# Fills written as 32-bit words chunk by chunk, the first keys fetched from ScalarE's queue, and the recurrence begun on half a chunk

## What is computed

```python
# layer 0
qkv = ln(x) @ w_qkv.T                      # 16 heads of 16
x += softmax(mask(q @ k.T * scale)) @ v @ w_proj.T
x += cross_attention(ln(x), ctx) @ Wo      # 77 keys
x += sum_e gate[e] * (ln(x) @ We[e] + be)  # 8 experts, top 2 by weight
# layer 1
xi = ln(x) @ Wi.T + bi
h = tanh(xt + h @ Wh.T + bh)               # lax.scan over the 1024 positions
x += hs
x += cross_attention(ln(x), ctx) @ wo + bo
x += gated experts (512 shared and 16 x 64 routed hidden units)
```

## Time and profile before

| | us |
|---|---|
| median of 3 runs | 1586.08 |
| lowest and highest of them | 1584.55, 1588.29 |
| the profiled execution's own time | 1593.49 |
| its span, from first to last instruction | 1591.9 |

### The profile page before, as it was taken

One profiled execution on the slowest core, in us unless ns is written; L12 is line 12 of the kernel. 1 busy time (PEld: TensorE's weight loads), 2 busy tenths in 40 slices (PEclk: granted clock), 3 DMA queues, 4 the chain that ended last, 5 costly groups with the idle time before them and its releaser, 6 DMA issues.

```text
span 1591.9 us, 49074 instructions
## 1 busy us (share of the span) xinstructions
PE 1529.6 (96%) x20210; PEld 1055.7 (66%) x20210; DVE 821.7 (52%) x2568; ACT 595.8 (37%) x2778; POOL 38.1 (2%) x60
## 2 busy tenths in 40 slices
PE   5498799999999999999999999999999999999998
PEld 4365267766777776767777777776766667666555
DVE  6746734387751179665212555753464433633264
ACT  1133151624237732422777555212522235322220
POOL 1100000000000000000000000000000000000000
PEclk9699789999999999999999998999989999999999
DMA  7324100110000020000001131000000010000100
GB/s 215 68 88 85 31 2 1 24 36 3 2 2 3 12 41 9 2 2 2 9 4 30 62 103 30 1 1 2 16 2 2 15 36 2 2 2 19 31 1 14
DMA packets 45472, 40.23 MB, mean 25 GB/s; under 512 B 9723, under 2 KB 44486, under 8 KB 45254
## 3 DMA queue, kind: packets, MB, share of 16 engines
q1 hardware_dynamic: 45254, 37.11, 9.9%
HBM read 25.81 MB, written 10.80 MB: 23 GB/s over the span
## 4 chain that ended last, share of the span: by engine, by line
PE 91%; DVE 6%; DMA 1%; issue 1%; ACT 0%; SPq 0%; DVEq 0%; ACTq 0%
PE b L509 20%; PE b L528 12%; PE b L1583 8%; PE b L1363 7%; PE b L1635 6%; PE b L993 5%; PE b L964 4%; PE b L734 4%; PE b L909 3%; PE b L690 3%; DVE mx L918 3%; PE b L1244 3%; PE b L1219 2%; PE b L451 2%; PE b L645 2%; PE b L493 1%
## 5 line engine op out<-in xcount | busy, mean ns | idle before, releaser
L509 PEld LDWEIGHTS b<-hp,whp 128*128 128x128 f16 x12276 | 481.0, 96 | 251.0 <-ACT hp L554 147.9
L509 PE MATMUL b<-hp,whp 128*128 128x2 f16 x12276 | 534.4, 165 | 2.0 <-DVE hp L560 0.8
L560 DVE TENSOR_TENSOR hp<-hist,hp 128x4 f16<-128x4 f32 x1023 | 165.7, 162 | 494.2 <-ACT hist L555 484.5
L554 ACT ACTIVATE hp<-b 128x4 f16<-128x4 f32 x1024 | 178.8, 175 | 536.6 <-PE b L509 525.0
L528 PE MATMUL b<-whp 128*128 128x512 f16 (+7 forms) x1038 | 256.0, 348 | 0.0
L918 DVE TENSOR_REDUCE mx<-b 128x1 f32<-128x512 f32 (+3 forms) x304 | 188.2, 657 | 5.4 <-PE b L912 4.8
L978 ACT ACTIVATE vp<-b 128x512 f32<-128x512 f32 x288 | 170.6, 603 | 25.0 <-PE b L967 13.3
L555 ACT ACTIVATE hist<-b 128x4 f32<-128x4 f32 x1024 | 178.8, 175 | 0.0
L1583 PE MATMUL b<-vp,heads 128*128 128x512 f16 x576 | 164.4, 379 | 0.0
L1363 PE MATMUL b<-we,xT 128*128 128x256 f32 x512 | 126.6, 391 | 0.0
L909 PE MATMUL b<-heads 128*128 128x512 f16 (+3 forms) x384 | 112.8, 332 | 7.1 <-DVE mx L918 3.7
(11 more groups left out here) (202 smaller groups left out, 1594.6 us busy)
## 6 DMA issues: line engine op xcount, KB each, us to landing
x_qs<-qx_scr SPq DMA_DIRECT2D x48, 128.0 KB
qx_scr<-xq_pair SPq DMA_DIRECT2D x16, 256.0 KB, 2.1
heads<-q_scr SPq DMA_DIRECT2D x24, 128.0 KB, 4.4
heads<-k_scr SPq DMA_DIRECT2D x48, 64.0 KB, 2.5
x<-in_x SPq DMA_DIRECT2D x8, 256.0 KB, 6.1
we<-in_L_ffn_We SPq DMA_DIRECT2D x2, 1024.0 KB
q_scr<-tail SPq DMA_DIRECT2D x8, 256.0 KB, 3.3
k_scr<-tail SPq DMA_DIRECT2D x8, 256.0 KB, 2.2
```

The source lines that it names most:

```text
L509: return pe.matmul(self.z(t)[:, m], self.w.whp[:, a, k, m * P:(m + 1) * P], self.g.hp16[:, (t - 1) % 2, part, k, :], start=False, stop=Tru ...
L554: act.activation(self.g.hp16[:, t % 2, 0], self.z(t), ACT.Tanh, scale=1 / LIFT).then_inc(self.s["hi_ready"], 1)
L560: v.tensor_tensor(self.g.hp16[:, t % 2, 1], self.g.hist[:, :, :, t % (4 * HALF)], self.g.hp16[:, t % 2, 0], ALU.subtract).then_inc(self.s[ ...
```

## The change

- **Fills.** Ones for the keys are written as 32-bit words (`ONES16` is the float whose bits are two 16-bit ones), in 8 memsets of 1024 words, one for each chunk and batch row, in place of 4 memsets of 4096 16-bit elements; `load_k` of chunk c waits for the fills of chunks 0 to c alone. The cross attention's key zeros and query ones are words too. The values' ones (`fill_v`) go only to the columns that need them. Small rows are filled first; the fills of later chunks and the cross attention's come after the first chunk's fourth `qk_part2`.
- **Transfers.** The 12 transfers of the first chunk's keys are issued from ScalarE's queue. Four kinds of SyncE's transfers (the weights of the recurrence and of the experts, the second layer's, and the cross attention's key rows and keys) are placed behind them in the plan.
- **Recurrence.** `start` waits for two stored tiles and does the products of half 0 alone; half 1 gets its 12 pieces inside the steps of half 0, every eighth step as the later halves do.
- **Ranks.** Norm, projections and values of layer 0 rank at 200c (AHEAD) in place of 1000c. n3 and its store rank at 45, before the experts' 50, not behind them at 60. The first pass may be at most 3 banks ahead of `self_highest` (FIRST_BANKS).
- Costs in the planner's list are adjusted to the above.

The diff, without the lines that only give names to the 32-bit views:

```diff
+FIRST_BANKS = 3
+AHEAD = 200
+
+ONES16 = (1 + 0x3C00 / 2 ** 23) / 2 ** 7
...
         self.piece_at = {HALF * (h - 1) + 16 + 8 * i + (1 - parity): (h, parity, m, k, i)
-                         for h in range(2, NH) for i, (parity, m, k) in enumerate(self.pieces)}
-        self.clear_at = {HALF * (h - 1) + 2 + parity: (h, parity) for h in range(2, NH) for parity in range(2)}
+                         for h in range(1, NH) for i, (parity, m, k) in enumerate(self.pieces)}
+        self.clear_at = {HALF * (h - 1) + 2 + parity: (h, parity) for h in range(1, NH) for parity in range(2)}
         st.ops["pe"]["idle"] = self.idle
-        st.add("pe", "start", self.start, 1, 6.0, lambda i: rank)
+        st.add("pe", "start", self.start, 1, 3.0, lambda i: rank)
...
     def start(self, pe, _):
-        pe.wait_ge(self.norm.s["stored"], 4)
+        pe.wait_ge(self.norm.s["stored"], 2)
         pe.wait_ge(self.w.s["lifted"], 1)
         pe.wait_ge(self.w.s["b_in"], 1)
         pe.wait_ge(self.w.s["row_in"], 1)
-        for h in range(2):
-            for parity, m, k in self.pieces:
-                last = self.inject(pe, h, parity, m, k, first=h == 0 and m == 0 and k == 0)
+        for parity, m, k in self.pieces:
+            last = self.inject(pe, 0, parity, m, k, first=m == 0 and k == 0)
         last.then_inc(self.s["started"], 1)
...
         if t - 2 in self.clear_at:
             h, parity = self.clear_at[t - 2]
-            pe.wait_ge(self.s["zeroed"], 2 * (h - 2) + parity + 1)
+            pe.wait_ge(self.s["zeroed"], 2 * (h - 1) + parity + 1)
...
-        if h in (3, 4):
+        if h == 3:
             act.wait_ge(self.s["started"], 1)
-        if h >= 5:
-            act.wait_ge(self.s["injected"], h - 4)
+        if h >= 4:
+            act.wait_ge(self.s["injected"], h - 3)
...
-        self.proj = Projection(st, "qk", 2 * KD, xT, [(c, w, ln) for c in range(NK)], block, rank, room.pair)
+        self.proj = Projection(st, "qk", 2 * KD, xT, [(c, w, ln) for c in range(NK)], block, lambda c: AHEAD * c + 10, room.pair)
...
-        st.add("pe", "self_v", self.make_v, 2 * NH * KD, 0.43, lambda i: chunk_of_tile(i // KD) + 0.095,
+        st.add("pe", "self_v", self.make_v, 2 * NH * KD, 0.43, lambda i: AHEAD * (i // KD // TC) + 10.095,
                opens=lambda i: ("self_v", i // KD) if i % KD == 0 else None)
-        st.add("act", "self_vkeep", self.keep_v, 2 * NH, 0.38, lambda j: chunk_of_tile(j) + 0.12,
+        st.add("act", "self_vkeep", self.keep_v, 2 * NH, 0.38, lambda j: AHEAD * (j // TC) + 10.12,
                closes=lambda j: ("self_v", j))
-        st.add("sp", "self_load_q", self.load_q, NK, 5.0, lambda c: rank(c) + 0.21, after=8.0)
-        st.add("sp", "self_load_k", self.load_k, NK, 7.5, lambda c: rank(c) + 0.21, after=8.0)
+        st.add("sp", "self_load_q", self.load_q, NK, 4.4, lambda c: rank(c) + 0.21, after=8.0)
+        st.add("act", "self_load_k0", lambda act, _: self.load_k(act, 0), 1, 7.0, lambda _: rank(0) + 0.21, after=6.0)
+        st.add("sp", "self_load_k", lambda sp, i: self.load_k(sp, i + 1), NK - 1, 7.5, lambda i: rank(i + 1) + 0.21,
+               after=8.0, behind=[("self_load_k0", lambda i: 1)])
         st.add("pe", "self_first", self.first_pass, len(self.items),
                lambda i: self.items[i][2] * (0.0535 * self.items[i][4] + 0.01) + 0.06 * self.items[i][2] * self.is_diagonal(i),
-               lambda i: chunk_of_tile(self.items[i][0]) + 0.22, opens=lambda i: ("self_first", i))
+               lambda i: chunk_of_tile(self.items[i][0]) + 0.22, opens=lambda i: ("self_first", i),
+               behind=[("self_highest", lambda i: i - FIRST_BANKS + 1)])
...
-        sp.wait_ge(self.w.s["ks_ones"], 2 * B)
+        sp.wait_ge(self.w.s["ks_ones"], B * (c + 1))
...
-        st.add("v", name + "_zero", self.zero, 2, 1.2, early, behind=first)
-        st.add("v", name + "_one", self.one, 4, lambda i: (0.4, 1.0, 1.0, 0.4)[i], lambda i: early(i // 3), behind=first)
+        st.add("v", name + "_zero", self.zero, 2, 1.4, early, behind=first)
+        st.add("v", name + "_one", self.one, 4, lambda i: (0.5, 1.2, 1.2, 0.5)[i], lambda i: early(i // 3), behind=first)
...
-        st.add("sp", name + "_rows_k", self.rows_k, 2, 5.2, early, after=4.0)
-        st.add("sp", name + "_load_k", self.load_k, 2 * B, 3.8, lambda i: early(i // B), after=5.0)
+        st.add("sp", name + "_rows_k", self.rows_k, 2, 5.2, early, after=4.0, behind=later)
+        st.add("sp", name + "_load_k", self.load_k, 2 * B, 3.8, lambda i: early(i // B), after=5.0, behind=later)
...
-        v.memset(self.layers[layer].ks.rearrange("p b h t -> p (b h t)"), 0.0).then_inc(self.s["zeroed"], 1)
+        v.memset(self.layers[layer].ks_words, 0.0).then_inc(self.s["zeroed"], 1)
...
-            v.memset(self.qs[:, half * (i - 1):half * i].rearrange("p h n -> p (h n)"), 1.0).then_inc(self.s["oned"], 1)
+            v.memset(self.qs[:, half * (i - 1):half * i].rearrange("p h n -> p (h n)").bitcast(F32), ONES16
+                     ).then_inc(self.s["oned"], 1)
...
-        ln1 = ChunkNorm(st, "n1", lambda i: (g.x_in[i // TC], 32), tile_rank(0, 0), xn1,
+        ln1 = ChunkNorm(st, "n1", lambda i: (g.x_in[i // TC], 32), lambda j: j // TC * AHEAD, xn1,
...
-                               lambda n: when(*order[n]) + 30, cross_room, [("fill", lambda i: 2)])
+                               lambda n: when(*order[n]) + 30, cross_room, [("fill", lambda i: 7), ("qk_part2", lambda i: 4)],
+                               [("self_load_k0", lambda i: 1)])
...
-        ln3 = ChunkNorm(st, "n3", lambda i: (experts.s["mixed"], (E0 + 1) * (i + 1)), tile_rank(0, 60),
+        ln3 = ChunkNorm(st, "n3", lambda i: (experts.s["mixed"], (E0 + 1) * (i + 1)), tile_rank(0, 45),
...
         def fill(v, i):
-            if i < 2:
-                v.memset(attn.qs[:, H // 2 * i:H // 2 * i + H // 2].rearrange("p h n -> p (h n)"), 0.0
-                         ).then_inc(s["qs_zeros"], 1)
-            elif i < 6:
-                b, half = (i - 2) // 2, (i - 2) % 2
-                v.memset(attn.ks[:, b, H // 4 * half:H // 4 * (half + 1)].rearrange("p h n -> p (h n)"), 1.0
-                         ).then_inc(s["ks_ones"], 1)
-            elif i == 6:
+            if i == 0:
                 v.memset(rw.lift_row[:], LIFT).then_inc(s["row_in"], 1)
-            elif i == 7:
+            elif i == 1:
                 v.memset(wx0.ones16[:], 1.0).then_inc(s["rows"], 1)
+            elif i == 2:
+                v.memset(wx1.one_row[:], 1.0).then_inc(s["row_in"], 1)
+            elif i < 5:
+                v.memset(heads[:, 8192 + 2048 * (i - 3):8192 + 2048 * (i - 2)], 0.0).then_inc(s["qs_zeros"], 1)
             else:
-                v.memset(wx1.one_row[:], 1.0).then_inc(s["row_in"], 1)
+                c, b = (i - 5) // B, (i - 5) % B
+                v.memset(heads[:, 4096 * b:4096 * (b + 1)].rearrange("p (r t) -> p r t", r=H // 2)[
+                    :, :, P * c:P * (c + 1)], ONES16).then_inc(s["ks_ones"], 1)
 
         def fill_v(v, i):
-            if i < 2:
-                v.memset(attn.va[:, NT // 2 * i:NT // 2 * (i + 1)].rearrange("p t w -> p (t w)"), 1.0
+            if i == 0:
+                v.memset(attn.va[:, :, 0:H * VW].rearrange("p t (h w) -> p t h w", w=VW)[:, :, :, DH], 1.0
                          ).then_inc(s["va_ones"], 1)
+            if i == 1:
+                v.memset(attn.va[:, :, H * VW:VP], 1.0).then_inc(s["va_ones"], 1)
...
-        st.add("sp", "load", load, 5, 2.0, lambda i: -3900 + 100 * i, after=5.0)
-        st.add("sp", "load_second", load_second, 3, 2.5, lambda i: (-3400, 190, 990)[i], after=5.0)
+        st.add("sp", "load", load, 5, 2.0, lambda i: -3900 + 100 * i, after=5.0,
+               behind=[("self_load_k0", lambda i: int(i > 2))])
+        st.add("sp", "load_second", load_second, 3, 2.5, lambda i: (-3400, 190, 990)[i], after=5.0,
+               behind=[("self_load_k0", lambda i: 1)])
         st.add("sp", "load_whole", load_whole, 2, 0.7, lambda j: 1000, after=12.0)
-        st.add("v", "fill", fill, 9, lambda i: (1.95, 1.95, 1.95, 1.95, 1.95, 1.95, 0.1, 0.1, 0.1)[i], lambda i: 10.12,
-               behind=[("fill_v", lambda i: 2)])
-        st.add("v", "fill_v", fill_v, 4, lambda i: (2.0, 2.0, 0.3, 0.3)[i], lambda i: 2)
+        st.add("v", "fill", fill, 5 + B * NK, lambda i: 0.2 if i < 3 else 2.0 if i < 5 else 1.1,
+               lambda i: 1.0 if i < 3 else 10.12 if i < 7 else 70.0,
+               behind=[("qk_part2", lambda i: 4 if i >= 7 else 0)])
+        st.add("v", "fill_v", fill_v, 4, lambda i: (0.4, 0.4, 0.3, 0.3)[i], lambda i: 2)
...
-        st.add("act", "n1_store", store1, 2 * NH, 0.35, tile_rank(0, 0.7), closes=lambda i: ("n1", i))
+        st.add("act", "n1_store", store1, 2 * NH, 0.35, lambda j: j // TC * AHEAD + 0.7, closes=lambda i: ("n1", i))
...
-        st.add("act", "n3_store", rnn.store_input, 2 * NH, 0.35, tile_rank(0, 60.7), closes=lambda i: ("n3", i))
```

(1 more changed line is left out.)

11 lines of the change are left out of this document (7 added, 4 removed).

## The result

The changed kernel takes 1571.54 us (median of 4 runs, 1566.34 to 1574.74). The kernel before took 1587.18 beside it (4 runs, 1584.55 to 1590.94). The ratio is 0.9897, with a 95% interval of 0.9862 to 0.9931: faster by 16 us, where the forecast said 42. The profiled execution took 1570.91 us, its span is 1569.2.

The account below looks back on a forecast made before the run. It took the end to be set by chunk 3 passing layer 0 (1057 us), then 367 steps and 129 us, with a 20 us hole at the head. 28 + 8 + 8 - 2 = 42 us off 1586.1 gave 1544, range 1528 to 1560.

Parts of the forecast that it names:

- The rival of the moved hole: After 82 us new lists leave new holes; only about a third of the sum arrives: 12 us, 1574 us; 13%.
- The three gains: Earlier head 28 us, half a chunk first 8 us, and the first pass's bank limit 8 us.
- the 2 that were taken off for costs: Less room ahead of VectorE in first passes and two more PSUM clears at steps 2 and 3: 2 us lost.
- Nothing in it has a date of its own: Line of chunks from 82 to 1057 us: each released by the one before, so the head's 28 us survive.
- head: Faster fills and earlier key loads bring the first maximum from 81.77 to 49 us; 28 us at the end.
- half chunk first, with n3's rank: Step 657 released 14.2 us earlier because two stored tiles suffice; bounds 0 and 14 us, 8 taken.
- banks: First pass limited to 3 of 5 banks, so experts of chunks 1 and 2 begin earlier; 8 us, at most 24.7.
- the sign given for the banks: In the profile after, fillers under 10 us in both stretches ahead of the experts of chunks 1 and 2.
- the weights in the way of the keys: Rival: 2.6 MB of weights pass before the first keys land; head gives 18 in place of 28, 1554 us; 12%.
- The start on half a chunk: First tanh 14 to 19 us earlier, worth nothing at the end because the break at step 145 absorbs it.
- The slower rival: First pass with 3 banks starves, VectorE waits at each maximum; gain gone or time up to 1623 us; 5%.
- the signs to look for: Profile after: key loads 34 to 44 us, first maximum 46 to 52, first tanh 225 to 240, step 657 1000 to 1025.

Follow-up runs that it names:

- the head alone and the guard moved: Changed kernel with ranks, bank limit, n3 and recurrence start as before, and the wait for the second layer's cross-attention values moved to step 102: 1565.64 us, ratio 0.985.
- the same head: Changed kernel keeping only the new fills and transfers; ranks, bank limit, n3 and recurrence start as before, wait still ahead of step 0: 1617.22 us, ratio 1.0179.
- 1559.73: Changed kernel with projections ranked at 1000c, no bank limit, and the wait for the second layer's values moved to step 102: 1559.73 us, ratio 0.983.
- the version at 1554.51: Changed kernel with layer 0's norm, projections and values ranked at 1000c again, all else as changed, three banks included: 1554.51 us, ratio 0.9802.
- two banks and the guard moved: Changed kernel with ranks at 1000c, two banks for the first pass, and the wait for the second layer's values moved to step 102: 1544.1 us, ratio 0.9733.
- the weights early: Changed kernel with the weights of the recurrence and experts not placed behind the first key loads: 1568.19 us, ratio 0.9869.
- the run with two banks: Changed kernel with ranks at 1000c and two banks for the first pass instead of three: 1544.61 us, ratio 0.9746.

## Why the forecast was wrong

**The failed step** is a term put at nothing without a reason: the ranks at 200c stand in the change and have no place in "28 + 8 + 8 - 2 = 42". They cost 17 us (1571.54 against 1554.51), and the intervals of the two ratios are apart. The rows that go with it are those of chunk 1: projections of later chunks stand between its first-pass products. The rival of the moved hole gave 1574 and came nearest. Its reason against itself, that projections "rank behind chunk 0's own work", looked at the wrong chunk: chunk 1's first pass ranks at 1000 and more, and projections of chunks 2 and 3 at 410 and 610 pass it.

The rest of the error is one of sizes. The three gains measure 33 us for 44 forecast, so 42 less 16 is made up of 17 for the ranks and 11 for the gains, less the 2 that were taken off for costs.

**"Nothing in it has a date of its own"** was the reason for letting the head's gain pass whole through the line of chunks. For the lists with the head alone and the guard moved it comes out: 23 us are gained at the first maximum (58.4 for 81.8), 25 and 26 at the last scores of chunks 2 and 3, and 27 at step 657. As a statement on the kernel it is false all the same. By the guard the recurrence can't begin before the projections of the last chunk are made, and with the guard in its place the same head gives 1617 us. In the kernel before, the last self values were made at 140 us and the second layer's values at 146, long ahead of the first tanh at 277.9; so the wait never showed in its trace, and could be read only in the code. That they were early because TensorE had nothing else to do in the hole that the change closes is likely by the order of the lists, but no run shows it. In the changed kernel the guard is not what costs the 17 us. The ranks at 200c do a real thing there: they keep the projections in time for the guard. But the limit of three banks does it too, and both together are one too many.

**The other terms:**

| term | forecast | measured |
|---|---|---|
| head | 28 | 22.2 (1587.86 - 1565.64), guard moved |
| half chunk first, with n3's rank | 8 | 5.9 (1565.64 - 1559.73), guard moved; not apart from 0 by the intervals |
| banks | 8 | 15.6 with two (1559.73 - 1544.1), guard moved; about 5 with three (1559.73 - 1554.51), not apart from 0 |
| ranks at 200c | none | -17.0 (1554.51 - 1571.54) |

With three banks that is 22 + 6 + 5 - 17 = 16 us. It must come out so, because each row begins where the one above it ends; the sum is a way of sharing out the 16 us and no proof. Its third step also crosses from the guard moved to the guard in its place. That should cost little, since step 657 has a break of 44 us in the version at 1554.51, and moving the guard changed nothing with two banks. A term depends on the lists that it is measured in, so the table is one order of the edits and not a law: n3's rank is worth 17.7 us in one pair of lists and -5 in another (1566.54 against 1571.54, the intervals overlap). Two of the forecast's terms were also weaker than they looked. The middle of 0 and 14 less 1 is 6, not 8. And the sign given for the banks, fillers under 10 us ahead of the experts of chunks 1 and 2, did not come: they are 14.59 us from 380 to 410 and 13.14 from 650 to 680.

No term stood for the granted clock. Its median was 0.973 in the kernel before, 0.977 to 0.978 in the changed one, 0.982 with the head alone and the guard moved, and 0.985 with two banks and the guard moved. At 1.5 us for each 0.001, an estimate, a good half of the head's 22.2 us and of the 15.6 us of two banks goes with the clock. TensorE stood idle and at 0.50 from 40 to 60 us before, so a part of that is the hole itself. How much of the rest is an effect of the order of work, no run shows.

**The head's size.** The first maximum was forecast for 49 and came at 60.1 (57.0 with the weights early), 21.7 us earlier than before and not 32.8. The keys account for 3 us of this: the last of them was issued at 39.4 and had landed by 49.7 at the latest, for 46.5 forecast. The rest is in TensorE's list. Its products for the second layer's keys (L63) stand ahead of chunk 0's first pass and wait until 57.9 for the second layer's bias, which SyncE issues only at 51.18, behind the weights of the experts (its two transfers hold the queue for 4.54 us from 40.33) and of the second layer (one of them holds it for 4.25 us). This load was placed behind the keys by the change itself, and I had given that no price. Ahead of it VectorE and ScalarE also sit 5.1 and 4.8 us on the weights of the recurrence, ahead of the norms that they have to do. With the weights early the bias is issued at 40.13 and the first maximum comes at 57.0, so the same wait is shorter and not gone.

The Trainium skill ("DMA: Bandwidth & Descriptors", Issuing engines are not separate DMA queues) says that transfers started by several engines run on the same 16 DMA engines and interleave, and that a second queue saves only the time of issuing. The rows fit that, with the engines busy 1.00 from 40 to 60 and landings of 8.3 us for 2.4, but no run shows it by itself. The rival that the forecast built on it, the weights in the way of the keys, is refuted as it stood: with the weights long landed the keys took 7.7 us at the median, and the first maximum gained 3 us, not 10.

**The half chunk.** The start on half a chunk was priced at nothing and is worth nothing (1569.93 against 1571.54). The two expert tiles that now come behind step 657 were feared to cost up to 14 us, and the 405 us after it are the same as before. The fillers did not give the room, as the forecast had it: they are 78.5 us for 79.55. In that stretch 11.6 us of expert products (36 of L1371) are new, and 24 products of layer 1's gated experts, 6.1 us, lie elsewhere; the stretch's clock was 0.98 for 0.97.

**The slower rival**, a first pass starved by three banks, is refuted by the run with two banks, the fastest but for the moved guard. A slower kernel was near all the same, from a cause not on the list: without the limit and the ranks, the same head gives 1617.

**Of the signs to look for** in the profile after, the key loads (34 to 44), the first tanh (225, forecast 225 to 240), the 129 us and the fills came as forecast. Step 657 (1035 for 1000 to 1025), the first maximum and the fillers did not. "The first maximum early but chunk 1's scores no earlier" was the sign given for a moved hole, and it is what the trace shows.

## What to carry to other kernels

When the order of all work is planned anew, a gain at one place is only as good as the next wait in the new lists: look for guards that protect reused memory, which cost nothing in the old trace because their condition happened to come early. Give every edit of a change a term, ranks and limits too, and time such edits together and apart, since two cures for one wait (a limit on one kind, a higher rank for another) can each be right alone and cost 17 us together. Give a price to what the change moves back as well: a load put behind the urgent ones can be awaited by work that stands ahead of them in another engine's list. With lists held fixed an edit of the head can be priced (7.6 us for 8.6 here); with lists that move, compare whole versions, and put the granted clock beside each time.
